# First stage of a four-layer graph network: zeros and x are copied in 2 KB pieces, a portion per group, and TensorE counts a group late

## The reference

```python
def _hconv(x, W, b, src, dst):
    x = x @ W
    deg_n = segment_sum(ones, src, N_NODES)              # 50000
    deg_e = segment_sum(ones, dst, N_HEDGES)             # 10000: edges with a larger dst drop out
    Dinv = where(deg_n > 0, 1 / deg_n, 0); Binv = where(deg_e > 0, 1 / deg_e, 0)
    he = Binv[:, None] * segment_sum(x[src], dst, N_HEDGES)
    out = Dinv[:, None] * segment_sum(he[dst], src, N_NODES)
    return out + b
h = relu(_hconv(h, W1, b1, src, dst))
return _hconv(h, W2, b2, src, dst)
```

## Time and profile before

| | us |
|---|---|
| three runs: median (lowest to highest) | 3168.17 (3165.29 to 3176.83) |
| the profiled execution: its own time | 3174.55 |
| its span | 3172.7 |
| first phase, from the start to the next phase's first VectorE instruction | 703.2 |
| busy in the whole span: PE, DVE, ACT, POOL | 2096.2, 2151.0, 1683.3, 1592.1 |

### The profile page before, as it was taken

One profiled execution on the slowest core, in us unless ns is written; L12 is line 12 of the kernel. 1 busy time (PEld: TensorE's weight loads), 2 busy tenths in 40 slices (PEclk: granted clock), 3 DMA queues, 4 the chain that ended last, 5 costly groups with the idle time before them and its releaser, 6 DMA issues. The chain is left out here.

```text
span 3172.7 us, 48341 instructions
## 1 busy us (share of the span) xinstructions
PE 2096.2 (66%) x10165; PEld 1480.5 (47%) x10165; DVE 2151.0 (68%) x8784; ACT 1683.3 (53%) x4590; POOL 1592.1 (50%) x1489
## 2 busy tenths in 40 slices
PE   0667236738775778777874778787885666665675
PEld 0245112525553656666651334343444556664565
DVE  1665346738885989887966777777755544443999
ACT  0666100218883656565655888988874444442222
POOL 1324245340006888888827555655616777774000
PEclk9987567869995767776666999999998888877999
DMA  9433851539997878887836999999976555554998
GB/s 321 115 80 69 262 157 49 120 61 302 324 327 258 248 238 253 244 245 233 248 83 202 286 286 283 295 284 287 293 189 208 183 181 185 182 176 133 314 320 278
DMA packets 493386, 698.11 MB, mean 220 GB/s; under 512 B 66393, under 2 KB 357428, under 8 KB 485834
## 3 DMA queue, kind: packets, MB, share of 16 engines
q1 hardware_dynamic: 413086, 486.50, 49.4%
q0 software_dynamic: 63360, 130.75, 15.4%
q10 hardware_dynamic: 16784, 79.36, 7.0%
HBM read 420.86 MB, written 328.79 MB: 236 GB/s over the span
## 5 line engine op out<-in xcount | busy, mean ns | idle before, releaser
L290 POOL DMA_INDIRECT xs<-x_d,table_src x400 | 385.4, 963 | 356.2 <-DVE x L1624 137.6
L290 POOL DMA_INDIRECT xs<-n_d,srcI x200 | 247.4, 1237 | 325.1 <-DVEq L1273 269.8
L290 POOL DMA_INDIRECT xd<-n_d,dstI x200 | 226.1, 1131 | 60.9 <-issue 53.6
L290 POOL DMA_INDIRECT xd<-x_d,table_dst x200 | 209.1, 1046 | 65.1 <-issue 65.1
L1982 PE MATMUL bank<-xs,same 128*128 128x129 f32 x400 | 109.5, 363 | 178.5 <-ACT sums L1951 93.1
L1843 POOL DMA_INDIRECT r_d<-rd,out_row x200 | 196.7, 983 | 60.9 <-issue 60.6
L1779 PEld LDWEIGHTS bank<-nmsg,same 128*128 128x128 f32 x400 | 61.6, 194 | 263.9 <-ACT sums L1711 204.7
L1779 PE MATMUL bank<-nmsg,same 128*128 128x128 f32 x400 | 100.2, 333 | 124.8 <-ACT sums L1711 67.9
L285 ACT ACTIVATE root<-tmp,eps 128x4 f32<-128x4 f32 (+3 forms) x253 | 76.8, 304 | 199.3 <-DVE tmp L261 199.1
L575 PE MATMUL bank<-mask,h 128*128 128x512 f32 x160 | 101.3, 792 | 123.0 <-DVE mask L969 123.0
L266 DVE RECIPROCAL rs<-root 128x4 f32<-128x4 f32 (+3 forms) x253 | 52.3, 207 | 183.3 <-ACT root L285 148.7
(11 more groups left out here) (395 smaller groups left out, 7083.2 us busy)
## 6 DMA issues: line engine op xcount, KB each, us to landing
n_d<-T SPq DMA_DIRECT2D x98, 528.0 KB, 3.8
nt<-n_d SPq DMA_DIRECT2D x49, 1056.0 KB, 7.0
r<-r_d SPq DMA_DIRECT2D x98, 520.0 KB, 5.7
bc<-dst_d SPq DMA_DIRECT2D x170, 256.0 KB, 4.8
r_d<-nv SPq DMA_DIRECT2D x49, 528.0 KB, 7.9
v_d<-nv SPq DMA_DIRECT2D x49, 528.0 KB, 8.0
nv<-v_d SPq DMA_DIRECT2D x49, 528.0 KB, 4.1
x_d<-x SPq DMA_DIRECT2D x100, 256.0 KB, 4.0
```

What stands on the lines that cost most here:

```text
L290: pool.indirect_dma_start(out=out, out_offset=None, in_=table, in_offset=bass.IndirectOffsetOnAxis(ap=index, axis=0)).then_inc(s, 16)
```

## The change

Zeros. The 16 DMAs at the start become 5 on ACT's queue (portions 0 to 4, 3200 rows each, in pieces of 8 rows, 4 KB). SP issues portion 5 and, behind every `load_bc(g)` of the first convolution, portion g + 6, in pieces of 4 rows (2 KB). A rest follows in `behind`. x. ACT's 13 copies go; behind every `load_bc(g)` of the second convolution SP issues a copy of 5120 rows (2.6 MB) in 2 KB pieces, and a rest in `behind`. `pieces` gives a copy three dimensions: `b` (the outer one), `a` = 2, and the piece.

Counting. `hot` and `lows` have 6 buffers instead of 2, `hot_ready`, `lows_ready` and `col_ready` start 3 higher, and TensorE counts what was made for the group before (`counted_first`, `counted_rest`, `counted_before`). `combine` shares its buffer with `mask`.

Order. The second pass of VectorE is cut into `mixing` (combine, later), `reached`, `addressed` (row numbers for the scatter, a group later), `counted` and `inverted`; `mixing(0)` comes ahead of the copy of `across`. On TensorE `combined(g)` follows `hyperedges(g)` directly, where before it was that of the group before, and on ScalarE `additions(g)` follows `rows_of_edges(g)`. SP issues `load_back` of the first two groups before the last two `store_sums`. In the second convolution POOL issues the gathers of rows before it waits for `meta_out`, and the four of `meta_d` behind it. `steps_behind` is computed ahead of `set_up`.

```diff
-ZERO = 3168
+ZERO = 3200
+XC = 2560
-        sum1_d = dram("sum1_d", (NN + G * P, D))
-        x1_d = dram("x1_d", (NX, D))
+        sum1_d = dram("sum1_d", (ZERO * (NGE + 12), D))
+        x1_d = dram("x1_d", (2 * XC * (NGE + 6), D))
...
+            def pieces(ap, rows=4):
+                return ap.rearrange("(a b c) f -> b a (c f)", a=2, c=rows)
+            def clear(eng, first, count, rows=4):
+                eng.dma_start(pieces(sum1_d[bass.ds(first, count), :], rows), pieces(t["x"][N:N + count, :], rows)).then_inc(zeroed, 16)
+            def copy_x(eng, to_first, from_first, count):
+                eng.dma_start(pieces(x1_d[bass.ds(to_first, count), :]), pieces(t["x"][bass.ds(from_first, count), :])).then_inc(
+                    x_copied, 16)
...
                         def load_bc(g, s):
...
+                            if conv == 0:
+                                clear(sp, (g + 6) * ZERO, ZERO)
+                            else:
+                                copy_x(sp, g * (2 * XC), (g % 10) * (2 * XC), 2 * XC)
...
-                        lagged_by_two(sp, n, load_bc, store_sums)
-                        for s in range(2):
-                            hold("sp", sp, sums_out[conv][s], n * 8 + 16)
...
+                        load_bc(0, 0)
+                        load_bc(1, 1)
+                        if conv == 0:
+                            clear(sp, 5 * ZERO, ZERO)
+                        with sp.Fori(2, n - 1, 2) as i:
+                            load_bc(i, 0)
+                            store_sums(i - 2, 0)
+                            load_bc(i + 1, 1)
+                            store_sums(i - 1, 1)
+                        load_back(0, 0)
+                        load_back(1, 1)
+                        store_sums(n - 2, 0)
+                        store_sums(n - 1, 1)
+                        bounded(sp, m, behind)
+                        bounded_from(sp, 2, n, load_back)
...
                             for j in range(G):
-                                gather(pool, er[:, s, j, :], t["x"] if conv == 0 else sum1_d, ix[:, s, j:j + 1], er_in[conv][s])
-                                if conv == 1:
+                                gather(pool, er[:, s, j, :], t["x"] if conv == 0 else sum1_d[0:NN + G * P, :], ix[:, s, j:j + 1], er_in[conv][s])
+                            if conv == 1:
+                                pool.wait_ge(meta_out, 16)
+                                for j in range(G):
                                     gather(pool, ms[:, s, j, :], meta_d, ix[:, s, j:j + 1], ms_in[s])
...
-                        lagged_thirds(pe, n, hyperedges, combined, counted)
-                        combined(n - 1, 1)
+                        def slot(g, s):
+                            hyperedges(g, s)
+                            counted_first(g, s)
+                            combined(g, s)
+                            counted_rest(g, s)
+                        hyperedges(0, 0)
+                        combined(0, 0)
+                        slot(1, 1)
+                        bounded_from(pe, 2, n, slot)
+                        counted_first(n, 0)
+                        counted_rest(n, 0)
...
-                    for k in range(16):
-                        act.dma_start(sum1_d[k * ZERO:(k + 1) * ZERO, :].rearrange("(p r) f -> p (r f)", p=96),
-                                      t["x"][N:N + ZERO, :].rearrange("(p r) f -> p (r f)", p=96)).then_inc(zeroed, 16)
+                    for k in range(5):
+                        clear(act, k * ZERO, ZERO, 8)
...
-                            for k in range(NX // COPY):
-                                act.dma_start(x1_d[k * COPY:(k + 1) * COPY, :].rearrange("(p r) f -> p (r f)", p=P),
-                                              t["x"][k * COPY:(k + 1) * COPY, :].rearrange("(p r) f -> p (r f)", p=P)).then_inc(x_copied, 16)
...
+                        def addressed(g, s):
+                            hold("dve", dve, e["landed"], g + 1)
+                            nc.vector.tensor_copy(to[:, s, :], to_all[:, bass.ds(g * G, G)]).then_inc(e["to_ready"], 1)
...
+                        def slot(g, s):
+                            reached(g, s)
+                            if conv == 0:
+                                addressed(g - 1, 1 - s)
+                            counted(g, s)
+                            inverted(g, s)
+                        dve.wait_ge(e["sums_ps"], n + 1)
+                        mixing(0, 0)
+                        dve.wait_ge(e["across_ps"], 1)
...
+                        bounded_from(dve, 2, n, lambda g, s: (mixing(g, s), slot(g, s)))
```

More of the change, by code:

```diff
@@ L328, in build @@
             er, h = (sb(n, [P, 2, G, D], F32, c) for n in ("er", "h"))
-            mask, combine = (sb(n, [P, 2, G, G * P], F32, c) for n in ("mask", "combine"))
+            mask = combine = sb("mask", [P, 2, G, G * P], F32, c)
             st = sb("st", [P, 2, G, 6], F32, c)
@@ L414, in _ @@
                     n = groups_of_low(sp)
+                    sp.wait_ge(set_up, 1)
+                    m = steps_behind(sp)
                     for s in range(2):
@@ L577, in sums, with counted_before, counted_and_sums @@
                             last.then_inc(e["sums_ps"], 1)
-                            if conv == 1:
-                                for k in range(3):
-                                    destinations(g * 3 + k, (s + k) % 2)
-                        bounded(pe, n, sums)
+                            if conv == 0:
+                                sources(g * 2 + 5, 5)
+                        def counted_before(g, s):
+                            for k in range(3):
+                                destinations(g * 3 + (k + 1), 3 - s * 3 + k)
+                        def counted_and_sums(g, s):
+                            counted_before(g, s)
+                            sums(g, s)
+                        if conv == 0:
+                            bounded(pe, n, sums)
+                        else:
+                            sums(0, 0)
+                            counted_and_sums(1, 1)
+                            bounded_from(pe, 2, n, counted_and_sums)
                         pe.wait_ge(e["sums_in"], n + 2)
@@ L665, in _, with signs @@
                     act.wait_ge(set_up, 1)
-                    def signs(k, b, at):
-                        hold("act", act, hot_used, k + 1)
+                    def signs(k, b, at, free):
+                        hold("act", act, hot_used, k + free)
                         for j in range(G):
@@ L686, in relus @@
                             if conv == 0:
-                                signs(g * 2, 0, g)
+                                signs(g * 2, 4, g, 5)
                                 act.wait_ge(e["mixed"], g + 1)
@@ L700, in relus @@
                             if conv == 0:
-                                signs(g * 2 + 1, 1, n + g)
+                                signs(g * 2 + 1, 5, n + g, 5)
                         def sums(g, s):
@@ L986, in stages, with mixing @@
                             ends()
-                        dve.wait_ge(e["across_ps"], 1)
-                        width = D + 1 if conv == 0 else D
-                        nc.vector.tensor_copy(across[:, 0:width], side[:, 0:width]).then_inc(e["across_in"], 1)
-                        def reached(g, s):
-                            dve.wait_ge(bcd_in[conv][s], pre_count(g, s, 1))
-                            dve.wait_ge(e["he_ps"], g + 1)
-                            nc.vector.tensor_scalar(reach[:, s, :], bcd[:, s, :], across[:, D + 1:D + 2],
-                                                    K0[:, bass.ds(g + Z_VALID, 1)], ALU.is_equal, ALU.mult).then_inc(e["reach_ready"], 1)
+                        def mixing(g, s):
                             dve.wait_ge(bcs_in[conv][s], pre_count(g, s, 1))
@@ L1030, in reached, with counted, slot @@
                             nc.vector.reciprocal(binv[:, s, :], binv[:, s, :]).then_inc(e["binv_ready"], 1)
-                            for k in range(2):
-                                if conv == 0:
-                                    sources(n * 2 + g * 3 + (k + 1), (s + k + 1) % 2, n * 2 + g * 3 + (k + 1))
-                                else:
-                                    destinations(n * 3 + g * 2 + k, k)
-                            if conv == 0:
-                                dve.wait_ge(e["landed"], g + 1)
-                                nc.vector.tensor_copy(to_all[:, bass.ds(g * G, G)], later[:, 2, :])
-                                nc.vector.tensor_copy(to[:, s, :], later[:, 2, :]).then_inc(e["to_ready"], 1)
-                                dve.wait_ge(e["to_ready"], g + 1)
-                        bounded(dve, n, reached)
+                        def counted(g, s):
+                            if conv == 0:
+                                for k in range(3):
```

(19 more changed lines are left out.)

137 lines of the change are left out of this document (78 added, 59 removed).

## The result

The changed kernel takes 2993.8 us (median of 4 runs, 2982.5 to 3012.7), the kernel before beside it 3168.35 (4 runs); the ratio is 0.9451, 95% interval 0.9399 to 0.9503. The profiled execution took 2990.95 us, span 2989.1.

What follows compares the result with a forecast made beforehand. Two walls of DMA, at the start and before the second convolution, beside passes with room were taken to bound the edited stage; six terms summed to -170 us, 3004.6 profiled and 2998 in the runs, range 2965 to 3050.

Steps and rivals of the forecast that it cites:

- Term 1: Start: fewer zeros, in 4 KB pieces, ahead of TensorE's loads let small loads through sooner; -57 us.
- the 45 us: Start: zero copies holding SP's issues beyond 45 us would show the prediction wrong.
- Term 2: First pass: deferred zeros on SP's queue, DMA and ScalarE both full, later counting without effect; +13 us.
- +4: First pass: bc(2), behind portions 7 and 5, comes at 68 where the mask wants it at 64; +4 us.
- Terms 3 and 4: Second pass, reordered, period 10.2 us: -37 us; wall before second convolution, no x copy in the way, 27 us left: -66.
- Term 5: Third pass: GpSimd sets 12.4 or 12.5 us a group, the copy of x hidden; -13 us.
- Term 6: Fourth pass: combined follows its own group's he, first scatter 11.5 us behind across, not 21.5; -10 us.
- B: Start: first 8.2 MB of zeros go through fewer engines, ten; bc(2) 13 us later; 3011 us, chance 0.17.
- C: First and third pass: copies fill them, 6.5 and 10.4 us per portion, first scatters late; 3040 us, chance 0.14.
- D: Whole stage: TensorE keeps 2.4 GHz because its gaps close, every term takes its good end; 2960 us, chance 0.08.
- E: First and third pass: walls only change place because 2 KB pieces are slow; 3230 us at 100 GB/s, chance 0.04.
- F: Start and first pass: SP's issues stick behind any full queue, loads are not freed; 3155 to 3180 us, chance 0.02.

Runs made afterwards that it cites:

- the ring open: Changed kernel with first-pass second count ahead of the sums again, marks and signs in four buffers in turn, or both: 2988.3, 2988.3 and 2977.0 us.
- the pipeline part: Changed kernel with zeros and x copied as in the kernel before, in big pieces from ScalarE's queue: 3115.7 us, 0.9838 of the kernel before.
- the last four runs: Changed kernel again and three further versions, made together when all kernels took longer: 3317.5, 3305.0, 3291.7 and 3311.9 us; kernel before 3437.9 to 3501.3.
- The old copies with the ring open: Changed kernel with second count ahead of the sums, four buffers of marks, and zeros and x copied as in the kernel before: 3078.6 us (one run).
- both edits: Changed kernel with first-pass second count ahead of the sums again and marks and signs in four buffers in turn: 2977.0 us, ratio 0.9404.

## Why the prediction came out as it did

The time was 2993.8 where 2998 was forecast, and the sum -170 stands against -174.5 in the medians. That closeness is partly luck: the stage itself gave 164.6 us, and the rest came from code that the change doesn't touch. By its steps:

- **Term 1, the start (-57; measured -57.7).** Right in its mechanism: a small load waits for a short packet. The size was right in part by luck. The sum had packets of 16.9 KB and 0.80 us; the trace has 33.9 KB and 1.58 us, with which the same sum would give an estimated 29 us for the first weight matmul and not 43, and neither is the 38.32 measured. It lacked the issuing engine, which short pieces hold up; that never showed in ScalarE's work, since only five portions were left to it. On SyncE's queue it did: the issues of portions 7 and 5 were held until 46.8 us, which is past the 45 us that the prediction named as a sign of being wrong.
- **Term 2, the deferred zeros (+13; measured +20.4).** This is the step that failed, and not in size alone. "TensorE's later counting gives nothing here, since it is not the limit" was wrong: the later counting closed a ring through buffer 5 and set a period of 10.1 to 10.2 us. "DMA needs 7.9 us per group against ScalarE's 7.76: both full" described the limit that came second. With the ring open the copies cost 10 to 12 us, near the 13 forecast; and the forecast's "+4" for a late third `bc` was then two waits of 7.2 us in all. In the changed kernel that `bc` landed at 68.0, where the prediction had placed it, and cost nothing, because the mask came no sooner. TensorE was busy 32 of 40 us in this pass, and from that I took it to have room; I did not write down what each buffer's next writer waits for.
- **Terms 3 and 4, the second pass and wall (-37 and -66; measured -102.2 together).** Right in size: the degree work stands 35.4 us nearer to the first pass's end, and 26.8 us from there to `dinv` (27 forecast). But the wall's term was worked out as if only the copies stood in the way, and 25 us of it came with the pipeline part while the old copies were still there. The period forecast at 10.2 is read from the first scatters of three groups, 10.4 and 10.1 apart:

```profile
233.24 1.55 POOL L539 DMA_INDIRECT sum_d<-add,to  x1 [2.85 <-issue]
...
243.60 1.55 POOL L539 DMA_INDIRECT sum_d<-add,to  x1 [3.24 <-issue]
...
253.66 1.55 POOL L539 DMA_INDIRECT sum_d<-add,to  x1 [2.93 <-issue]
```

- **Term 5, the third pass (-13; measured -14.0).** Right in size by luck, 12.4 us a group. The copies take 3 to 5 us of it, where the forecast had them hidden; GpSimd without them is at 11.5 to 11.8, better than its forecast 12.4 to 12.5, and the two errors cancel.
- **Term 6, the fourth pass (-10; measured -11.1).** Right, 10.8 us to the first scatter (11.5 forecast), with the x copy 2 us from deciding it.
- **Rivals.** B's mechanism is there by the DMA shares, and its 13 us are not. C's mechanism, copies that fill a pass, showed in the second pass when x was put there, and for some 0.4 us a group in the third. D did not happen: the clock fell to 0.88 in the first pass. E and F did not either.
- **Left open.** The profiled pair differs by 183.6 us and the stage by 164.6. The other 19 us lie in code that the change doesn't touch, most of them between 1000 and 1740 us of the kernel before. From the next phase's first transposed rows to the end, eight profiles outside the last four runs took 2436.4 to 2446.8 us, the kernel before 2458.2 and the pipeline part alone 2453.6. The old copies with the ring open are among the eight (2438.8), so the copies' form is not it; how much is one execution's clock was not separated.

## What to carry to other kernels

When work is moved behind something on one engine, write down for every buffer it frees who writes it next and what that writer holds up: the engine's busy share (TensorE's was 78% of this pass before the change) says nothing about a ring. Ask of a hidden cost which limit hides it, since two limits don't add: opening the ring gained 10 us and not 20, because the copies were waiting behind it. And a bulk copy in short pieces frees the other queues' small loads but ties up the engine that issues it, so give it to the engine with nothing to do, in few portions.

## What was unexpected of the hardware

- Sixteen DMAs of 1.6 MB took ScalarE 10.55 us to issue in 16.9 KB pieces and 86.45 us in 2 KB pieces.
- While both queues had work, SyncE's and ScalarE's moved the same number of packets, 575 and 575 in 60 us, with 0.18 and 19.52 MB in them.
- Outer dimension 200 in 4 KB pieces left engines empty (share 0.81 over 24 us), 400 in 2 KB pieces did not (1.00), at 279 and 301 GB/s.
- The granted clock of the first pass was not read off TensorE's busy share: with the ring open and no copies it was 1.00 at 32.17 busy of 40 us (106 matmuls), with the ring closed 0.83 at 31.93 of 40 us (80 matmuls), with copies or without. Over the whole pass it was 0.94 with both edits and the copies, 0.88 in the changed kernel. Whether the clock fell because of the ring or the ring turned slower because of the clock was not separated.
- The changed kernel took 2993.8 us at first and 3317.5 in the last runs. In its two profiles the edited stage took 538.6 and 543.7 us and what follows it 2450.5 and 2768.0, at a mean granted clock of 0.84 and 0.79. What made the later runs longer is not shown.
